# Layer 1's cross-attention: the order of VectorE's two pieces of work in a step

## What is computed

```python
def _L1_xattn_ref(encoded, decoded, Wq, bq, Wk, bk, Wv, bv, gamma, beta):
    q = decoded @ Wq.T + bq
    k = encoded @ Wk.T + bk
    v = encoded @ Wv.T + bv
    qk = jnp.einsum('bhqd,bhkd->bhqk', q, k)
    attn = jax.nn.softmax(qk, axis=-1)
    z = jnp.einsum('bhqk,bhkd->bhqd', attn, v)
    z = z.reshape(B, Sq, D)
    x = z + decoded
    return (x - mu) * jax.lax.rsqrt(var + LN_EPS) * gamma + beta
```

## Time and profile before

| What | us |
|---|---|
| Median of 3 runs | 1818.31 (1815.8 to 1818.58) |
| The profiled execution's own time | 1824.05 |
| Its span, first to last instruction | 1822.3 |
| PE busy in the span | 1506.7 (83%) |
| DVE busy | 1197.1 (66%) |
| ACT busy | 971.0 (53%) |
| POOL busy | 533.7 (29%) |

### The profile page before, as it was taken

One profiled execution on the slowest core, in us unless ns is written; L12 is line 12 of the kernel. 1 busy time (PEld: TensorE's weight loads), 2 busy tenths in 40 slices (PEclk: granted clock), 3 DMA queues, 4 the chain that ended last, 5 costly groups with the idle time before them and its releaser, 6 DMA issues. The chain is left out here.

```text
span 1822.3 us, 27871 instructions
## 1 busy us (share of the span) xinstructions
PE 1506.7 (83%) x8907; PEld 823.0 (45%) x8908; DVE 1197.1 (66%) x4538; ACT 971.0 (53%) x2014; POOL 533.7 (29%) x466
## 2 busy tenths in 40 slices
PE   5859999999975688888878879999978982289997
PEld 3512222222224566666656533333346761056665
DVE  6978888888808999999983267777535568211111
ACT  2835766777674666666655436666745551111111
POOL 1782000000002445655565541221202432421111
PEclk9958999999997899999999879999999995699999
DMA  7195324243000000000004654375020123521110
GB/s 219 58 232 66 43 39 104 38 88 47 1 27 1 1 1 1 1 1 1 2 19 78 132 127 63 48 126 108 1 93 4 19 41 100 183 73 43 47 41 6
DMA packets 116040, 106.02 MB, mean 58 GB/s; under 512 B 45811, under 2 KB 92987, under 8 KB 115902
## 3 DMA queue, kind: packets, MB, share of 16 engines
q1 hardware_dynamic: 110641, 93.83, 24.6%
q0 software_dynamic: 2640, 6.31, 0.9%
q10 hardware_dynamic: 2624, 4.19, 0.7%
HBM read 68.56 MB, written 36.41 MB: 58 GB/s over the span
## 5 line engine op out<-in xcount | busy, mean ns | idle before, releaser
L1128 DVE TENSOR_REDUCE arena<-banks 128x2 f32<-128x1024 f32 (+1 forms) x448 | 484.1, 1108 | 157.8 <-PE banks L944 103.1
L1049 ACT ACTIVATE arena<-banks 128x512 f32<-128x512 f32 (+3 forms) x896 | 435.4, 557 | 192.4 <-PE banks L983 188.0
L944 PE MATMUL banks<-arena 96*128 96x512 bf16 (+3 forms) x896 | 269.5, 377 | 44.8 <-DVE arena L1128 23.5
L983 PE MATMUL banks<-arena 98*128 98x512 bf16 (+3 forms) x896 | 263.9, 362 | 8.2 <-ACT arena L1049 7.8
L997 PE MATMUL banks<-arena 128*32 128x512 f32 (+3 forms) x1792 | 219.5, 562 | 1.2 <-ACT arena L1049 0.7
L2058 DVE MATCH_REPLACE8 arena<-arena 128x77 f32<-128x77 f32 x1024 | 213.9, 224 | 0.0
L944 PEld LDWEIGHTS banks<-arena 96*128 96x128 bf16 x896 | 72.6, 100 | 253.6 <-issue 110.3
L2916 DVE COPY arena<-banks 128x1024 f32<-128x1024 f32 x23 | 28.2, 1224 | 203.0 <-PE banks L2850 168.2
L983 PEld LDWEIGHTS banks<-arena 98*128 98x128 bf16 x896 | 83.3, 98 | 155.9 <-ACT arena L1049 87.3
L2050 DVE MAX8 arena<-arena 128x8 f32<-128x77 f32 x1024 | 149.7, 224 | 0.7
L1920 POOL TENSOR_SCALAR arena<-arena 128x256 f32<-128x256 f32 x32 | 17.9, 558 | 406.5 <-DVE arena L2038 406.5
(11 more groups left out here) (302 smaller groups left out, 2495.8 us busy)
## 6 DMA issues: line engine op xcount, KB each, us to landing
arena<-parts SPq DMA_DIRECT2D x192, 128.0 KB, 7.0
arena<-in_L_ffn_W SPq DMA_DIRECT2D x12, 1024.0 KB, 10.9
v<-arena SPq DMA_DIRECT2D x32, 256.0 KB, 3.2
arena<-v SPq DMA_DIRECT2D x16, 512.0 KB, 10.7
parts<-arena SPq DMA_DIRECT2D x12, 512.0 KB, 5.2
parts<-arena SPq DMA_DIRECT2D x16, 384.0 KB, 2.5
arena<-in_L_ffn_W ACTq DMA_DIRECT2D x4, 1024.0 KB, 7.0
arena<-sorted_rows SPq DMA_DIRECT2D x23, 129.0 KB, 2.2
```

Of the source, the lines that this page charges most:

```text
L944: mm = pe.matmul(bank[:, 0:w], qst[r][0:KS, j, i * P:(i + 1) * P], kst[r][0:KS, j, kb * BANK:kb * BANK + w], start=True, stop=not diag)
L983: pe.matmul(bank, kst[r][0:KM, j, kt * P:(kt + 1) * P], qst[r][0:KM, j, half * BANK + lo:(half + 1) * BANK], start=True, stop=True).then_i ...
L1049: act.activation(prob[:, gi % 2 * G + j, lo:BANK], PS[:, 4 + n % 3, 0:BANK - lo], ACT.Exp, scale=SCALE).then_inc(sem(s + "_exp"), 1)
L1128: dve.tensor_reduce(m2[u % 2][:, 2 * pair:2 * pair + 2, i, kb], PS[:, 2 * (n % 2):2 * (n % 2) + 2, 0:w], AX.X, ALU.max).then_inc(sem(s + " ...
```

## The change

DVE's two pieces at the head of a step change places: `normalize` of tile t-3 comes first, then `maxima` of tile t. The clamp stays last. Nothing is added or removed, and no other engine's list changes.

```diff
                 def body(dve, t, r):
                     o = 1 - r
+                    if inside(t - NLAG):
+                        normalize(t - NLAG, r if NLAG == 2 else o)
                     if inside(t):
                         if top:
                             largest(t, r)
                         else:
                             maxima(t, r)
-                    if inside(t - NLAG):
-                        normalize(t - NLAG, r if NLAG == 2 else o)
                     if not top and inside(t):
                         dve.wait_ge(sem(s + "_e"), t + 1)
```

## The result

The changed kernel takes 1830.01 us (median of 4 runs, 1828.6 to 1832.19), the kernel before 1817.99 us beside it (4 runs, 1815.8 to 1818.58). The ratio is 1.0067, with a 95% interval from 1.0055 to 1.0079. It is slower by 12.0 us, as was forecast (1830.3).

What follows compares the result with a forecast made beforehand. The prediction took a cycle through DVE, PE and ACT in layer 1's cross-attention, 7.43 us per step, as the bound. 11.8 us inserted plus 0.2 us at the stage's end gave 12.0 us: 1830.3 us, range 1825.3 to 1836.5.

Steps and rivals of the forecast that it cites:

- The ring: Layer 1's cross-attention: eviction, scores, weights' copy, exponential, clamp, next eviction set the 7.43 us step; `normalize` between clamp and eviction lengthens it.
- The slack of POOL's path: From eviction to exponential, POOL's reduction and subtraction end 0.08 us apart from PE's and ACT's path, so both bind.
- The sum: Insertion in 13 cross-attention steps: ten loop steps at 0.93 us, three written-out at 0.82 us, 11.8 us in all.
- The 13.1 us: Alternative total for the insertion: 1.01 us end to end in each of 13 steps, if DVE's instructions didn't overlap.
- The tail: Step 15 and the stage's end: PE's removed 2.90 us wait isn't worth its length; +0.2 us, between -2.2 and +0.6.
- Nothing behind the stage absorbs it: Layer norms, router and POOL's scatter all start from the stage's end, so the delay reaches the program's end in full.
- The clock: Rival in the loop: PE's idle ahead of the scores grows to 1.34 us and its clock falls; 14 us more, chance 0.09.
- `normalize` waiting at the head of the step: Rival: `normalize` waits for PE's `turn_context` and holds up the eviction, half a microsecond in 13 steps, 1836.8 us; chance 0.03.
- The other side: Rival: eviction has slack of 0.93 us or more, PE's work sets the step, loop cost 0; 1818.3 to 1816.1 us, chance 0.06.

Runs made afterwards that it cites:

- e1_loop: Kernel before, with `normalize` first only in the ten loop steps (4 to 13); 1827.48 us against 1819.02, ratio 1.0048.
- e3_between: Kernel before, with `normalize` moved between the eviction and the reduction of the new tile; 1828.82 us against 1819.02, ratio 1.0049.
- e8: Kernel before, with DVE's order eviction of tile t, `normalize`, clamp of tile t-1, reduction of tile t; 1807.35 us, ratio 0.9935.
- e2_step15: Kernel before, with `normalize` first only in step 15; 1820.24 us against 1819.02, ratio 1.0002.
- e9: Changed kernel plus an unused reduction over half of the heads between `normalize` and eviction in 13 steps; 1853.57 us, ratio 1.0191 to the kernel before.
- e5: Kernel before, with the clamp of tile t-1 at the end of DVE's step t and `normalize` ahead of the eviction; 1855.76 us, ratio 1.0168.
- e7_eviction_ahead: Kernel before, with DVE's order eviction of tile t, clamp of tile t-1, reduction of tile t, `normalize` of tile t-3; 1806.04 us, ratio 0.9929.
- e4_clamp_late: Kernel before, with the clamp of tile t-1 at the end of DVE's step t, behind eviction, reduction and `normalize`; 1864.59 us, ratio 1.0214.
- e6: Changed kernel plus one full unused reduction between `normalize` and eviction in 13 steps; 1869.89 us, ratio 1.0254 to the kernel before.

## Why the prediction was right

**The ring.** Right, point by point: `normalize` came out of idle time and onto the ring, and what it costs there is its length start to start. `e1_loop` shows that it is paid per step, `e3_between` that both paths were tied, and `e8` that `normalize` next to the eviction is free once the eviction isn't on the ring. The slack of POOL's path was read as 0.08 us; ACT's copy and the exponential overlap, and `e3_between` leaves nearly nothing of it.

**The sum.** 0.93 and 0.82 us per step were forecast; measured are 0.92 (8.34 against 7.43, and 8.35 in other pairs against 7.42) and 0.83 (8.21 against 7.38). For the 13 steps together the forecast was 11.8 us and the evictions give 125.49 - 113.85 = 11.6. The start-to-start gaps 0.20, 0.39 and 0.34 came out to the hundredth. The 13.1 us that the Trainium skill's section on the drain would have given, read by itself, is 1.5 us too much: L2429 starts 0.08 us before L2451 has ended (1445.36 against 1445.44).

**The tail** is the term that failed, in its sign. Forecast was +0.2 us, the four profiles show -0.7: 15.3 us from the last eviction to the layer norm instead of 16.0. The reasoning that the removed wait is replaced by the one for the last clamp was right. The sum for PE's slow matmuls left out a piece: `context` of the last tile, which ran slowly before,

```profile
1504.41 1.75 PE L2267 MATMUL banks<-arena 77*32 77x128 f32 x32
```

and takes 1.08 us after (1517.06, above). I had expected the clock to come back later, and it came back earlier against PE's work. The swap in step 15 isn't needed for that: in `e1_loop`, where step 15 has the order of before and its wait of 2.90 us, the same piece takes 1.08 us and the tail 15.2, and in `e2_step15`, with the swap in step 15 alone, 1.29 us and 15.6.

```profile
1506.27 0.84 PE L2276 MATMUL banks<-arena 128*128 128x128 f32 x4 [2.90 <-DVE arena L2451]
...
1514.22 1.08 PE L2267 MATMUL banks<-arena 77*32 77x128 f32 x32 [0.23 <-ACT arena L2327]
```

What decides where the clock comes back stays open. With the tail the stage gives 10.85 us. The measured 12.0 and 10.0 us of the two comparisons lie on either side, and their intervals both hold it; the first agreeing with the sum to the tenth is luck.

**Nothing behind the stage absorbs it.** Right: 313.9 and 308.0 us before, 313.1 and 307.3 after, long compared with long and short with short. The 0.7 us between them are no more than the short profiles of the other kernels differ (307.8 to 308.5).

**The clock.** It stayed at 1.00 as forecast, with PE busy for 81% and 1.32 us idle ahead of the scores. With 0.7 us more per step it fell in `e9`, so the chance of 0.09 was fair or somewhat low. The rival's price of 14 us was well sized: the stage of `e9` is 23.1 us longer than that of the changed kernel, of which 13 x 0.7 = 9.1 us are the inserted work, which leaves 14 us by this estimate. The Trainium skill's passage on PSUM queues and the clock ("TensorE: Matmul & The Clock Gate", "A second HAM failure mode: psum-queue depth-cycling") describes what `e9` shows, matmuls of 2.32 and of 4.00 us in turn; the changed kernel shows nothing of it.

**`normalize` waiting at the head of the step** didn't come true: at 1444.43 it has no bracket. It did in `e5`, where the rest of DVE's order was another.

**The other side,** a slack of the eviction of 0.93 us or more, would have needed PE to be the bound. It wasn't; `e7_eviction_ahead` had to be built for that.

## What to carry to other kernels

Ask of a piece of work not how long it is, but whether it stands on the ring that sets the step: before, 0.9 us of `normalize` was free behind the reduction, cost its full length ahead of the eviction, and was free again behind an eviction that had been taken off the ring (`e8`). To find the ring, write down every engine's order, not only the one that is edited; `e4_clamp_late` failed on PE's order, which it didn't touch. A single comparison of two variants can mislead too: `e5` against `e4` looks like proof that the swap can win, and the trace shows that another instruction had become faster. And in this kernel the idle time was worth most to the piece that another engine waits for: moving the eviction into it, as in `e7_eviction_ahead`, took 12.6 us off.

## What was unexpected of the hardware

**Some DVE instructions wait for POOL's.** The clamp, both of whose operands lie in SBUF, takes 0.80 us alone and 2.26 us when it starts during POOL's subtraction; in `e4_clamp_late` it ends 0.66 us after that one does (1439.71 against 1439.05). The statistics of `e4`'s line 2466 over 16 instances, min, median and max in ns:

```profile
L2466 DVE TENSOR_SCALAR arena<-arena x16: 791/2257/2262, 1386.7 to 1543.2; 128x1232 f32<-128x1232 f32 x16
```

An addition with two inputs in SBUF (`add_context`, 0.41 us alone) took 1.88 us beside the same subtraction in `e7_eviction_ahead`:

```profile
1478.58 2.27 POOL L2372 TENSOR_TENSOR arena<-arena 128x1232 f32<-128x1232 f32 x1 [3.79 <-DVE arena L2434]
...
1479.24 1.88 DVE L2476 TENSOR_TENSOR arena<-arena 128x256 f32<-128x256 f32 x1
```

`normalize`, which reads PSUM, isn't held up in the same place: its multiply takes 0.42 us beside POOL's subtraction at 1442.35. Where the clamp starts first, as in `e5` at 1402.94, it takes its 0.79 us, and POOL's subtraction, from 1403.11, takes 2.75 us instead of 2.27. The Trainium skill, "SBUF — State Buffer", section "Who interferes with whom", says that VectorE and GpSimd share a pair of ports, that a VectorE instruction with two inputs in SBUF, or one in a mode that uses both pairs of ports, contends for it with GpSimd, that the later one waits for the whole of the other, and that any other VectorE instruction isn't concerned. The addition and the multiply of `normalize` agree with it; so does the clamp if it runs in such a mode, which no trace shows.

**PE's clock fell behind idle spells of 2.0 us, but not behind each of them.** 1.32 us in each step of 8.34 us left it at 1.00. 2.03 us in each step of `e9` brought it to a mean of 0.88: the scores behind the first such spells took 2.32 us, those from 1423.84 on 3.6 to 4.0 us, and those at 1455.88 again 2.32. With 2.67 us in `e6` the mean is 0.87. Where between 1.32 and 2.03 us it begins wasn't tried. No run has a lone spell of 2 us, so it isn't shown either whether they have to recur.
